# Window attention on one core: channel layout, GpSimd key sums, seeded PSUM banks

## Chip, cores and metric

The kernel runs on one core of one Trainium2 chip. The metric is device time in microseconds, from the launch to the end, median of three runs. PE is TensorE, DVE VectorE, ACT ScalarE, POOL GpSimd, SP the engine that issues most DMAs; all data is float32.

## What is computed

The input `x` has 4 images of 128 channels and 32x32 pixels. It is group-normalised (32 groups of 4 channels), goes through an attention over windows of 2x2 positions (8 heads of 16 features) on the image and on its 2x2 average pool, and is added to the result. The `reshape` reads the channel-first array as if it were channel-last, so a window's tokens come from several channels.

```python
def window_attn(x, Wqkv, bqkv, scale, ws=WS, nh=NH):
    B, H, W, C = x.shape
    hg, wg = (H // ws, W // ws)
    hd = C // nh
    xw = x.reshape(B, hg, ws, wg, ws, C).transpose(0, 1, 3, 2, 4, 5)
    qkv = (xw @ Wqkv + bqkv).reshape(B, hg * wg, ws * ws, 3, nh, hd)
    q, k, v = jnp.transpose(qkv, (3, 0, 1, 4, 2, 5))
    attn = jax.nn.softmax(jnp.einsum('bgnqd,bgnkd->bgnqk', q, k) * scale, axis=-1)
    o = jnp.einsum('bgnqk,bgnkd->bgnqd', attn, v)
...
g = window_attn(xr, Wqkv, bqkv, scale) @ Wproj + bproj
l = xr.reshape(B, C, H, W)
l = l.reshape(B, C, H // 2, 2, W // 2, 2).mean(axis=(3, 5))
l = l.reshape(B, h, w, C)
l = window_attn(l, Wqkv, bqkv, scale)
...
l = jax.image.resize(lx + ly, (B, C, H, W), method='bilinear')
l = l.reshape(B, H, W, C)
return (g + l).transpose(0, 3, 1, 2)
...
x = x + _L0_conv_ref(_gn(x), L0_conv_Wqkv, L0_conv_bqkv, L0_conv_Wproj, L0_conv_bproj)
```

`lx` and `ly` are averages of the low result with its neighbour row and neighbour column.

## The kernel before

The work is cut into ten tiles of 128 windows (`TILES`): two halves of each image, and two low tiles, `(None, 0)` and `(None, 1)`, each with the pooled maps of two images. A tile has 512 tokens: 4 token places of 128 windows. Token 0 is taken from the other three before the key and value products (softmax does not notice a shift common to all keys), so that only 3 keys need work; key 0's score is zero and its value is added whole.

Each engine runs a list written out by hand (`ORDER`), strictly in its order, with semaphore waits between engines. The steps, by name and line:

- Two row loads per image (`xr`, L285 to L290 and L419 to L422), and a second load of x by channels (`xc`, L295) for the addition at the end. SP issues most, ACT some.
- `bn`, `mean`, `dev`, `var`, `gvar`, `std`, `off`: statistics of each image's two row sets, group means by a small matmul, and the inverse deviation on POOL (L350).
- `scale` (ACT, L431) and `norm` (POOL, L278; DVE for image 0) make the normalised tokens `xn`, less token 0. `pool` (POOL, L373, L379) and `low` (ACT, L441) make the pooled ones.
- `xt` and `lt` (PE, L644, L656) turn a tile so that features lie on the partitions; `xto` and `lto` copy it out of PSUM.
- `Q`, `K`, `V` (PE, L681, L672, L691): products with the weights. `Qo` copies the queries out with their bias.
- `M` (DVE, L542): 4 queries times 3 keys for every window, 1536 elements for each partition. `S` (PE, L713) sums them over the heads for a batch of two tiles. `X` (DVE, L550, L555) takes the maximum off, `E` (ACT) is the exponential, `D` (DVE, L562 to L573) sums the denominators, inverts, multiplies and turns the weights in blocks.
- `P` (DVE, L590): weights times values, again 1536 elements.
- `v0` (PE, L739) turns key 0's value into a PSUM bank for each of the 4 queries, and `O` (PE, L755) adds the 12 products of 4 queries and 3 keys, each turned by a transposing matmul. `Oo` (ACT, L477) copies the sum out.
- `low` (PE, L771) is the resize matrix times the low result, 5 matmuls for half an image; `out` (PE, L778) adds the projection; `res` (ACT or DVE) adds the bias and, on DVE, x; `add` (POOL, L410) adds x where ACT did it. SP stores each image, the last one in two parts.

In the trace an fp32 matmul has two records, a transpose one.

## Time and profile before

| | us |
|---|---|
| median of 3 runs | 93.77 |
| lowest, highest | 93.16, 94.08 |
| span of the profiled execution | 92.3 |
| PE busy | 79.7 |
| DVE busy | 61.6 |
| ACT busy | 36.6 |
| POOL busy | 26.9 |

The span goes from the first to the last instruction on the core; the run's time includes what lies around it. The profiled execution's own total is not printed, so its span is set beside the median: 1.5 us lie between them. The busy shares are means over the whole span; the views that follow split them by stage. Line numbers are those of the kernel before.

### The profile page before, as it was taken

To read this page: it belongs to the slowest core of one execution; us is meant where nothing else is said; L and a number is where in the kernel's file an instruction comes from. 1 tells how busy PE (TensorE), PEld (TensorE's weight loads), DVE (VectorE), ACT (ScalarE), POOL (GpSimd) and SP (SyncE) were. 2 spreads that over 40 slices of the span, in tenths; PEclk is the share of its full clock that TensorE was granted. 3 is DMA by queue.
4 is the path that set the end of the run, shared out by engine and by line. 5 is a ranking of instruction groups with operands and counts; after the bars stand their busy time and mean duration, and the time that the engine had idled before them with its cause. 6 is when DMAs were issued, how large, how long until landed. Compare 5 with 4: busy or idle time off the path is not lost.

```text
span 92.3 us, 1700 instructions
## 1 busy us (share of the span) xinstructions
PE 79.7 (86%) x620; PEld 62.0 (67%) x620; DVE 61.6 (67%) x101; ACT 36.6 (40%) x80; POOL 26.9 (29%) x50
## 2 busy tenths in 40 slices
PE   1936057999999999999999999999999999999900
PEld 1925053878574577876677968797799897797500
DVE  0072499597685999999999918999779465003240
ACT  0050005577849997734564331331533150222000
POOL 6845595267364444000000000320060005060000
PEclk9999999999999999999999999999999999999999
DMA  0999999920000000000000000000005000005056
GB/s 6 248 254 251 228 322 404 415 87 0 7 0 0 0 4 0 11 0 0 0 0 0 7 0 0 0 0 0 7 0 227 0 0 4 7 0 227 0 227 227
DMA packets 3464, 7.32 MB, mean 79 GB/s; under 512 B 896, under 2 KB 1152, under 8 KB 3456
## 3 DMA queue, kind: packets, MB, share of 16 engines
q1 hardware_dynamic: 2592, 5.84, 18.4%
q10 hardware_dynamic: 864, 1.38, 6.3%
q8 instruction: 5, 0.08, 0.3%
q14 instruction: 3, 0.02, 0.1%
HBM read 5.11 MB, written 2.10 MB: 78 GB/s over the span
## 4 chain that ended last, share of the span: by engine, by line
PE 74%; DMA 9%; ACT 3%; POOL 3%; DVE 2%; issue 2%; ACTq 2%; DVEq 1%
PE ot_ps L755 14%; PE q_ps L681 9%; PE v_ps L691 9%; DMA xr<-in_x 9%; PE k_ps L672 6%; PE job_ps L771 6%; PE s_ps L713 6%; PE ot_ps L739 5%; PE job_ps L778 5%; PE job_ps L644 4%; PE k_ps L771 2%; ACT xn L431 2%; PE job_ps L656 2%; PE k_ps L778 2%; ACT xt L447 1%
## 5 line engine op out<-in xcount | busy, mean ns | idle before, releaser
L542 DVE TENSOR_TENSOR qk<-q_sb,k_ps 128x1536 f32<-128x1536 f32 x10 | 17.3, 1737 | 2.7 <-ACT q_sb L460 2.7
L410 POOL TENSOR_TENSOR out_sb<-out_sb,xc 128x512 f32<-128x512 f32 x4 | 6.0, 1512 | 40.9 <-ACT out_sb L482 40.9
L590 DVE TENSOR_TENSOR pv<-prob_w,v_ps 128x1536 f32<-128x1536 f32 x9 | 15.7, 1739 | 0.7 <-PE ot_ps L755 0.7
L755 PEld LDWEIGHTS ot_ps<-ident,pv 128*128 128x128 f32 x120 | 13.7, 141 | 3.3 <-issue 3.0
L755 PE MATMUL ot_ps<-ident,pv 128*128 128x128 f32 x120 | 14.9, 273 | 0.0
L477 ACT ACTIVATE ot<-ot_ps,bias_qkv 128x512 f32<-128x512 f32 x10 | 6.9, 687 | 12.8 <-PE ot_ps L755 12.8
L497 DVE BATCH_NORM_STATS2 bn<-xr 128x6 f32<-128x512 f32 x8 | 5.5, 682 | 6.6 <-DMA xr<-in_x 6.6
L681 PE MATMUL q_ps<-xt,w_sb 128*128 128x512 f32 x16 | 9.3, 665 | 0.5 <-ACT xt L447 0.5
L691 PEld LDWEIGHTS v_ps<-w_sb,xt 128*128 128x128 f32 x64 | 7.9, 192 | 1.0 <-issue 1.0
L691 PE MATMUL v_ps<-w_sb,xt 128*128 128x128 f32 x64 | 8.5, 275 | 0.0
L278 POOL TENSOR_TENSOR xn<-xn 128x384 f32<-128x384 f32 x6 | 6.0, 1000 | 8.0 <-ACT xn L431 8.0
L713 PE MATMUL s_ps<-qk,head_sum 128*32 128x192 f32 x160 | 7.5, 329 | 0.0
L431 ACT ACTIVATE xn<-xr,offset,rstd 128x256 f32<-128x256 f32 x12 | 6.6, 598 | 1.2 <-POOL offset L357 1.2
L672 PE MATMUL k_ps<-xt,w_sb 128*128 128x384 f32 x16 | 7.0, 517 | 0.0
L771 PEld LDWEIGHTS job_ps<-ot,resize_sb 128*128 128x128 f32 x50 | 6.1, 192 | 0.8 <-issue 0.8
L771 PE MATMUL job_ps<-ot,resize_sb 128*128 128x128 f32 x50 | 6.5, 277 | 0.0
L713 PEld LDWEIGHTS s_ps<-qk,head_sum 128*32 128x32 f32 x160 | 4.7, 110 | 2.6 <-issue 1.6
L739 PE MATMUL ot_ps<-ident,v_sb 128*128 128x128 f32 x40 | 6.1, 274 | 0.0
L599 DVE SCALAR_TENSOR_TENSOR out_sb<-k_ps,bias_p,xc 128x256 f32<-128x256 f32 x4 | 1.8, 480 | 6.4 <-PE k_ps L778 6.3
L644 PEld LDWEIGHTS job_ps<-ident,xn 128*128 128x128 f32 x28 | 3.6, 152 | 3.5 <-issue 1.5
L783 PE MATMUL q_ps<-ident 128*128 128x128 f32 x16 | 4.1, 440 | 1.9 <-POOL ident L317 1.9
L739 PEld LDWEIGHTS ot_ps<-ident,v_sb 128*128 128x128 f32 x40 | 4.7, 141 | 1.4 <-issue 1.4
(81 smaller groups left out, 120.3 us busy)
## 6 DMA issues: line engine op xcount, KB each, us to landing
xc<-in_x SPq DMA_DIRECT2D x4, 512.0 KB, 11.1
out<-out_sb SPq DMA_DIRECT2D x3, 512.0 KB, 2.6
xr<-in_x ACTq DMA_DIRECT2D x5, 256.0 KB, 8.0
xr<-in_x SPq DMA_DIRECT2D x3, 256.0 KB, 7.2
resize_sb<-in_resize SPq DMA_DIRECT2D x1, 640.0 KB, 9.1
out<-out_sb SPq DMA_DIRECT2D x2, 256.0 KB, 2.4
w_sb<-in_L_conv_Wqkv SPq DMA_DIRECT2D x1, 192.0 KB, 4.7
wp_sb<-in_L_conv_Wproj ACTq DMA_DIRECT2D x1, 64.0 KB, 8.9
```

The lines of the kernel that those rows point to most:

```text
L431: ins = nc.scalar.activation(xn[:, b, k, 2 * r:2 * r + 2, :].rearrange("p s f -> p (s f)"), xr[:, b, r, k * 256:(k + 1) * 256], ACT.Identi ...
L477: nc.scalar.activation(ot[:, n, :], ot_ps[:, :], ACT.Identity, bias=bias_qkv[:, 2:3]).then_inc(ot_out, 1)
L542: nc.vector.tensor_tensor(qk[:, m % 2, :, :, n % 2, :], q, k, ALU.mult).then_inc(qk_done, 1)
L590: nc.vector.tensor_tensor(to, p, v, ALU.mult).then_inc(pv_done, 1)
L644: ins = nc.tensor.transpose(bank(job)[:, j * P:(j + 1) * P], xn[:, b, k, j, :], ident[:, :])
L672: nc.tensor.matmul(k_ps[n % 2][:, 0:KEYS * NW], w_sb[:, C:2 * C], tokens(n)[:, NW:], start=True, stop=True).then_inc(k_made, 1)
L681: nc.tensor.matmul(q_ps[:, :], w_sb[:, 0:C], tokens(n), start=True, stop=True).then_inc(q_made, 1)
L691: ins = nc.tensor.matmul(v_ps[n % 2][:, j * C:(j + 1) * C], tokens(n)[:, j * NW:(j + 1) * NW], w_sb[:, 2 * C:], start=True, stop=True, ski ...
L713: ins = nc.tensor.matmul(s_ps[rows, 64:256], head_sum[:, q, :], qk[:, m % 2, q, :, :, rows], start=(q == 0), stop=(q == WIN - 1), skip_gro ...
L739: nc.tensor.matmul(view[:, q // 2, q % 2], v0_sb[:, n % V0BUF, :], eye, is_transpose=True, start=(q == 0), stop=False, skip_group_check=True)
L755: ins = nc.tensor.matmul(view[:, q // 2, q % 2], pv[:, n % 2, q, k, :], eye, is_transpose=True, start=(sums == KEYS and q == 0), stop=last ...
L771: nc.tensor.matmul(view[:, column // 4, column % 2], resize_sb[:, i, :], low_ot, start=(i == used[0]), stop=True, skip_group_check=True)
```

## The change

x is loaded once, by channels, one DMA for each image, all on SP's queue, and the normalised x stays in that layout. Statistics are per channel, then per group of 4 channels. The turned tiles get the token order on PE (`T`), token 0 is subtracted after the turn (`df`, on POOL for tiles 4 to 9, on DVE for tiles 0 to 3), and every tile has buffers of its own for tokens and queries. The order of tiles differs. Names of steps after: `st`/`ps`/`pw`/`of` statistics, `nm` normalise, `pn` pooled maps, `xe` copy of turned tokens, `oo`/`om` copies of turned sums, `L` resize, `W` projection, `R` result. `sum_keys` (`H`, POOL) adds the second and third key's products to the first; for the two low tiles a third addition brings key 0's value. `O` then turns 4 sums in place of 12 products; tile 9 has no `H` and turns 12. For the low tiles `Om` turns the middle of the sums again, and `L` needs 4 matmuls. Key 0's value goes into the output bank by an ACT copy (`sd`, two instructions) and x with the projection's bias by another (`sx`), ahead of the matmuls that accumulate there. At the start three 512-column matmuls (`mark_banks`) mark those banks as written. `D` of batches 0 to 3 is split: `Ds` (POOL) two additions, `Dr` (DVE) reciprocal, `D` (POOL) product, `U` (DVE) turn; batch 4's stays on DVE, with two additions in place of the reduction. PSUM is dealt out by two tables, `A_BANK` and `B_BANK`.

```diff
-TILES = [(0, 0), (0, 1), (1, 0), (None, 0), (1, 1), (2, 0), (None, 1), (2, 1), (3, 0), (3, 1)]
+TILES = [(0, 0), (None, 0), (0, 1), (1, 0), (1, 1), (None, 1), (2, 0), (2, 1), (3, 0), (3, 1)]
...
+A_BANK = {
+    ("st", 0): 1, ("st", 1): 0, ("st", 2): 2, ("st", 3): 2, ("T", 0): 0, ("Q", 0): 3, ("K", 0): 0, ("T", 1): 1,
+    ("Q", 1): 3, ("K", 1): 2, ("V", 0): 2, ("V", 1): 3, ("O", 1): 1, ("Om", 1): 0, ("T", 2): 1, ("Q", 2): 1,
+    ("K", 2): 2, ("T", 3): 3, ("Q", 3): 3, ("K", 3): 0, ("V", 2): 2, ("V", 3): 0, ("T", 4): 1, ("Q", 4): 3,
+    ("K", 4): 1, ("T", 5): 1, ("Q", 5): 0, ("K", 5): 0, ("V", 4): 2, ("V", 5): 1, ("O", 5): 1, ("Om", 5): 2,
+    ("T", 6): 2, ("Q", 6): 1, ("K", 6): 0, ("T", 7): 1, ("Q", 7): 3, ("K", 7): 0, ("V", 6): 2, ("V", 7): 0,
+    ("T", 8): 3, ("Q", 8): 1, ("K", 8): 0, ("T", 9): 3, ("Q", 9): 2, ("K", 9): 3, ("V", 8): 1, ("V", 9): 3,
+}
+B_BANK = {
+    ("sd", 0): 1, ("sd", 2): 1, ("sd", 3): 1, ("sd", 4): 2, ("sd", 6): 0, ("sd", 7): 2, ("sd", 8): 2, ("sd", 9): 0,
+    ("sx", 0, 0): 2, ("sx", 0, 1): 0, ("sx", 1, 0): 0, ("sx", 1, 1): 1, ("sx", 2, 0): 1, ("sx", 2, 1): 2,
+    ("sx", 3, 0): 0, ("sx", 3, 1): 1,
+}
+PV = [2, 1, 3, 0, 0, 2, 3, 1, 3, 0]
+PV_BUFS = 1 + max(PV)
+ORDER = {
+    "PE": [
+        ("st", 0), ("st", 1), ("st", 3), ("T", 3), ("T", 2), ("T", 0), ("Q", 3), ("st", 2), ("T", 1), ("K", 3),
+        ("Q", 0), ("Q", 2), ("K", 2), ("zero",), ("K", 0), ("T", 4), ("Q", 1), ("S", 1), ("K", 1), ("T", 7), ("V", 3),
+        ("T", 9), ("T", 5), ("T", 6), ("T", 8), ("S", 0), ("V", 2), ("Q", 4), ("K", 4), ("Q", 5), ("Q", 7), ("Q", 9),
+        ("K", 5), ("V", 1), ("Q", 8), ("V", 0), ("S", 2), ("O", 2), ("K", 8), ("K", 9), ("Q", 6), ("V", 4), ("Om", 1),
+        ("O", 1), ("O", 3), ("K", 7), ("V", 5), ("S", 4), ("O", 0), ("V", 9), ("K", 6), ("L", 0, 1), ("L", 0, 0),
+        ("W", 0, 1), ("W", 0, 0), ("S", 3), ("V", 8), ("Om", 5), ("L", 1, 1), ("L", 1, 0), ("O", 4), ("W", 1, 0),
+        ("V", 7), ("W", 1, 1), ("O", 5), ("O", 9), ("O", 8), ("L", 3, 1), ("V", 6), ("W", 3, 1), ("L", 3, 0),
+        ("O", 7), ("W", 3, 0), ("L", 2, 0), ("L", 2, 1), ("O", 6), ("W", 2, 1), ("W", 2, 0),
+    ],
+    "DVE": [
+        ("bn", 0), ("bn", 1), ("ag", 0), ("ag", 1), ("ps", 0), ("ps", 1), ("bn", 3), ("of", 1), ("ag", 3), ("of", 0),
+        ("nm", 0, 0), ("bn", 2), ("df", 3), ("ag", 2), ("ps", 3), ("df", 2), ("df", 0), ("of", 3), ("ps", 2),
+        ("df", 1), ("of", 2), ("M", 3), ("M", 2), ("M", 0), ("X", 1), ("M", 1), ("Dr", 1), ("U", 1), ("P", 3),
+        ("X", 0), ("P", 2), ("Dr", 0), ("M", 4), ("U", 0), ("M", 5), ("P", 1), ("P", 0), ("M", 8), ("X", 2), ("M", 9),
+        ("M", 7), ("Dr", 2), ("X", 4), ("U", 2), ("P", 5), ("M", 6), ("P", 4), ("D", 4), ("U", 4), ("X", 3), ("P", 8),
+        ("Dr", 3), ("P", 9), ("U", 3), ("P", 7), ("P", 6), ("R", 3, 0),
+    ],
+    "ACT": [
+        ("sx", 0, 1), ("nm", 1), ("nm", 0, 1), ("xe", 3), ("pn", 1), ("xe", 2), ("pn", 0), ("xe", 0), ("Qo", 3),
+        ("xe", 1), ("pn", 3), ("pn", 2), ("Qo", 0), ("Qo", 2), ("nm", 3), ("xe", 4), ("nm", 2), ("Qo", 1), ("E", 1),
+        ("xe", 7), ("xe", 9), ("xe", 5), ("ve", 3), ("xe", 8), ("xe", 6), ("ve", 2), ("E", 0), ("Qo", 4), ("sd", 2),
+        ("Qo", 5), ("Qo", 7), ("Qo", 9), ("ve", 1), ("ve", 0), ("Qo", 8), ("sx", 0, 0), ("oo", 2), ("sd", 3),
+        ("Qo", 6), ("om", 1), ("oo", 1), ("oo", 3), ("E", 2), ("ve", 5), ("ve", 4), ("sd", 0), ("oo", 0),
+        ("sx", 1, 1), ("ve", 9), ("E", 4), ("R", 0, 0), ("sd", 4), ("R", 0, 1), ("sx", 1, 0), ("ve", 8), ("E", 3),
+        ("oo", 4), ("om", 5), ("R", 1, 0), ("sd", 8), ("ve", 7), ("sd", 9), ("R", 1, 1), ("oo", 5), ("sx", 3, 1),
+        ("oo", 8), ("oo", 9), ("sx", 3, 0), ("ve", 6), ("sd", 7), ("R", 3, 1), ("sx", 2, 0), ("oo", 7), ("sx", 2, 1),
+        ("sd", 6), ("oo", 6), ("R", 2, 1), ("R", 2, 0),
+    ],
+    "POOL": [
+        ("p1", 0), ("p2", 0), ("p1", 1), ("p2", 1), ("pw", 0), ("pw", 1), ("p1", 3), ("p2", 3), ("p1", 2), ("p2", 2),
+        ("keyb",), ("pw", 3), ("pw", 2), ("df", 4), ("Ds", 1), ("df", 7), ("D", 1), ("df", 5), ("df", 9), ("df", 8),
+        ("Ds", 0), ("df", 6), ("D", 0), ("H", 2, 0), ("H", 2, 1), ("H", 3, 0), ("H", 3, 1), ("H", 1, 0), ("H", 1, 1),
+        ("H", 1, 2), ("H", 0, 0), ("H", 0, 1), ("Ds", 2), ("D", 2), ("H", 5, 0), ("H", 5, 1), ("H", 5, 2),
+        ("H", 4, 0), ("H", 4, 1), ("Ds", 3), ("H", 8, 0), ("D", 3), ("H", 8, 1), ("H", 7, 0), ("H", 7, 1),
+        ("H", 6, 0), ("H", 6, 1),
+    ],
+}
+STORES = [0, 1, 3, 2]
+WARM = {("st", 0): 4, ("T", 0): 6}
...
         def _(sp):
-            sp.dma_start(xr[:, 0, 0, :], x_rows[0, 0]).then_inc(x0_first, 16)
+            sp.dma_start(xc[:, 0, :], x_chan[0]).then_inc(x_loaded[0], 16)
             sp.dma_start(w_sb[:, :], w_qkv).then_inc(w_loaded, 16)
-            for r in range(2):
-                sp.dma_start(xr[:, 2, r, :], x_rows[2, r]).then_inc(x_loaded[2], 16)
+            for b in range(1, B):
+                sp.dma_start(xc[:, b, :], x_chan[b]).then_inc(x_loaded[b], 16)
             for a in range(3):
                 sp.dma_start(bias_qkv[:, a:a + 1],
                              b_qkv[a * C:(a + 1) * C].rearrange("(p a) -> p a", a=1)).then_inc(bias_loaded, 16)
             sp.dma_start(bias_p[:, :], b_proj.rearrange("(p a) -> p a", a=1)).then_inc(bp_loaded, 16)
+            for h in range(2):
+                at = 2 * C + (1 - h) * 64
+                sp.dma_start(bias_mid[h * 64:(h + 1) * 64, :],
+                             b_qkv[at:at + 64].rearrange("(p a) -> p a", a=1)).then_inc(mid_loaded, 16)
+            sp.dma_start(wp_sb[:, :], w_proj).then_inc(wp_loaded, 16)
...
                 for k in range(2):
-                    result_written(sp, b, k)
+                    result_read(sp, b, k)
...
+            def less_token_0(n):
+                pool.wait_ge(token_0_out, nth("ACT", ("xe", n)))
+                rest = xt[:, n, NW:].rearrange("f (j w) -> f j w", j=KEYS)
+                nc.gpsimd.tensor_tensor(rest, rest, xt[:, n, 0:NW].unsqueeze(1).broadcast_to([P, KEYS, NW]),
+                                        ALU.subtract).then_inc(inputs_made[n], 1)
+            def denominators(m):
+                pool.wait_ge(exp_done, nth("ACT", ("E", m)))
+                done = nth("POOL", ("Ds", m))
+                e = expd[:, m % 2, :]
+                nc.gpsimd.tensor_tensor(pair_sum[:, m % 2, :], e[:, 0:128], e[:, 128:256], ALU.add).then_inc(pair_pool, 1)
+                pool.wait_ge(pair_pool, done)
+                nc.gpsimd.tensor_tensor(denom[:, m % 2, :], pair_sum[:, m % 2, 0:64], pair_sum[:, m % 2, 64:128],
+                                        ALU.add).then_inc(denom_pool, 1)
+            def divide(m):
+                pool.wait_ge(inv_pool, nth("DVE", ("Dr", m)))
+                if m >= 2:
+                    pool.wait_ge(turn_done, 2 * nth("DVE", ("U", m - 2)))
+                nc.gpsimd.tensor_tensor(prob[:, m % 2, :].rearrange("r (k w) -> r k w", k=KEYS),
+                                        expd[:, m % 2, 64:].rearrange("r (k w) -> r k w", k=KEYS),
+                                        inv[:, m % 2, :].unsqueeze(1).broadcast_to([P, KEYS, 64]),
+                                        ALU.mult).then_inc(prob_made[m], 1)
+            def sum_keys(n, i):
+                if i == 0:
+                    pool.wait_ge(pv_done, nth("DVE", ("P", n)))
                 else:
...
+            def scale_image(b, k=None):
+                act.wait_ge(offset_done, nth("DVE", ("of", b)))
+                at = (lambda t: t[:, b, :]) if k is None else (lambda t: halves(t, b, k))
+                nc.scalar.activation(at(xn), at(xc), ACT.Identity, bias=offset[:, b:b + 1],
+                                     scale=rstd[:, b:b + 1]).then_inc(normed_act, 1)
...
+            def value_0_out(n):
+                act.wait_ge(v_made, nth("PE", ("V", n)))
+                bank = a_bank(("V", n))
+                if is_low(n):
+                    nc.scalar.copy(v0[:, n, :], bank[:, KEYS * C:]).then_inc(v0_out, 1)
+                else:
+                    act.wait_ge(bias_loaded, 48)
+                    nc.scalar.activation(v0[:, n, :], bank[:, KEYS * C:], ACT.Identity,
+                                         bias=bias_qkv[:, 2:3]).then_inc(v0_out, 1)
+            def value_0_seed(n):
+                act.wait_ge(v0_out, nth("ACT", ("ve", n)))
+                b_free(act, ("sd", n))
+                to = b_bank(("sd", n))[:, :].rearrange("f (s m r c) -> f s m r c", s=2, r=2, c=GROUP)
+                at = v0[:, n, :].rearrange("f (m c) -> f m c", c=GROUP)
+                for s in range(2):
+                    ins = nc.scalar.copy(to[:, s], at.unsqueeze(2).broadcast_to([P, 32, 2, GROUP]))
+                ins.then_inc(seeded, 1)
...
+            def input_seed(b, k):
+                act.wait_ge(x_loaded[b], 16)
+                act.wait_ge(bp_loaded, 16)
+                b_free(act, ("sx", b, k))
+                nc.scalar.activation(b_bank(("sx", b, k))[:, :].rearrange("f (s h c) -> f s h c", s=2, h=2),
+                                     result_part(xc, b, k), ACT.Identity, bias=bias_p[:, 0:1]).then_inc(x_seeded, 1)
...
+            def less_token_0(n):
+                dve.wait_ge(token_0_out, nth("ACT", ("xe", n)))
+                nc.vector.tensor_tensor(xt[:, n, NW:].rearrange("f (j w) -> f j w", j=KEYS),
+                                        a_bank(("T", n))[:, NW:].rearrange("f (j w) -> f j w", j=KEYS),
+                                        xt[:, n, 0:NW].unsqueeze(1).broadcast_to([P, KEYS, NW]),
+                                        ALU.subtract).then_inc(inputs_made[n], 1)
...
             def divide(m):
+                dve.wait_ge(exp_done, nth("ACT", ("E", m)))
+                done = nth("DVE", ("D", m))
+                e = expd[:, m % 2, :]
+                nc.vector.tensor_tensor(pair_sum[:, m % 2, :], e[:, 0:128], e[:, 128:256], ALU.add).then_inc(pair_done, 1)
+                dve.wait_ge(pair_done, done)
+                nc.vector.tensor_tensor(denom[:, m % 2, :], pair_sum[:, m % 2, 0:64], pair_sum[:, m % 2, 64:128],
                                         ALU.add).then_inc(denom_done, 1)
+                dve.wait_ge(denom_done, done)
                 nc.vector.reciprocal(inv[:, m % 2, :], denom[:, m % 2, :]).then_inc(inv_done, 1)
+                dve.wait_ge(inv_done, done)
                 nc.vector.tensor_tensor(prob[:, m % 2, :].rearrange("r (k w) -> r k w", k=KEYS),
+                                        e[:, 64:].rearrange("r (k w) -> r k w", k=KEYS),
                                         inv[:, m % 2, :].unsqueeze(1).broadcast_to([P, KEYS, 64]),
+                                        ALU.mult).then_inc(prob_made[m], 1)
+            def invert(m):
+                dve.wait_ge(denom_pool, nth("POOL", ("Ds", m)))
+                if m >= 2:
+                    dve.wait_ge(prob_made[m - 2], 1)
+                nc.vector.reciprocal(inv[:, m % 2, :], denom[:, m % 2, :]).then_inc(inv_pool, 1)
+            def turn_weights(m):
+                dve.wait_ge(prob_made[m], 1)
                 for half in range(2):
                     nc.vector.transpose(
                         prob_w[:, m % 2, half, :].rearrange("w (q k h) -> w k q h", q=WIN, k=KEYS),
                         prob[:, m % 2, :].rearrange("r (k t w) -> r t k w", k=KEYS, t=2)[:, half]).then_inc(turn_done, 1)
...
+            def mark_banks():
+                for bank in b_ps:
+                    ins = nc.tensor.matmul(bank[:, :], ident[:, :], ident[:, :].unsqueeze(1).broadcast_to([P, 4, P]),
+                                           start=True, stop=True, skip_group_check=True)
+                ins.then_inc(banks_marked, 1)
+            def keep_warm(n):
+                for _ in range(n):
+                    nc.tensor.matmul(s_ps[:, 64:64 + P], ident[:, :], ident[:, :], start=True, stop=True,
+                                     skip_group_check=True)
...
+            def sum_values(n):
+                sums = [j for j in among("POOL", "H") if j[1] == n]
+                if sums:
+                    pe.wait_ge(keys_summed, nth("POOL", sums[-1]))
+                else:
+                    pe.wait_ge(pv_done, nth("DVE", ("P", n)))
+                left = [0] + list(range(1 + min(len(sums), 2), KEYS))
+                if is_low(n):
+                    a_free(pe, ("O", n))
+                    view = a_bank(("O", n))[:, :].rearrange("f (i l a r c) -> f r l i a c", i=2, l=KL, a=8, r=2)
                     eye = ident[:, :].rearrange("p (i a c) -> p i a c", i=2, a=8)
                 else:
+                    pe.wait_ge(seeded, nth("ACT", ("sd", n)))
+                    view = b_bank(("sd", n))[:, :].rearrange("f (s m r c) -> f r s m c", s=2, m=32, r=2)
+                    eye = ident[:, :].rearrange("p (m c) -> p m c", c=GROUP)
                 for q in range(WIN):
+                    for k in left:
+                        part = low_sum[:, TILES[n][1], q * C:(q + 1) * C] if is_low(n) else pv[:, PV[n], q, k, :]
+                        ins = nc.tensor.matmul(view[:, q // 2, q % 2], part, eye, is_transpose=True,
+                                               start=(is_low(n) and q == 0), stop=(k == left[-1]), skip_group_check=True)
+                ins.then_inc(ot_made, 1)
...
+                pe.wait_ge(x_seeded, nth("ACT", ("sx", b, k)))
+                pe.wait_ge(ot_out, nth("ACT", ("oo", low)))
+                pe.wait_ge(mid_out, nth("ACT", ("om", low)))
+                for h in range(2):
+                    for s in range(2):
+                        j = 4 * h + 2 * k + s
+                        if FIRST[j] == 64:
+                            values_at = mid[:, b // 2, b % 2 * P:(b % 2 + 1) * P]
+                        else:
+                            at = b % 2 * 256 + FIRST[j]
+                            values_at = ot[:, low, at:at + P]
+                        at = s * 256 + h * P
+                        nc.tensor.matmul(b_bank(("sx", b, k))[:, at:at + P], resize_sb[:, j, :], values_at, start=False,
+                                         stop=True, skip_group_check=True)
```

## Rows read from the trace of the kernel before

**Rows 1.** Busy us (count) of PE, PEld, DVE, ACT, POOL, then clock; 18 to 88.

```profile
span 92.3 us, 1700 instructions
18.00:88.00 70.00, 69.80 (x578) 54.08 (x578) 51.98 (x74) 32.68 (x73) 16.07 (x18) 1.00 0.06 22
```

**Rows 2.** Chain of work that ended last, PE's pieces: start us, us, records.

```profile
38.40 0.44 PE ot_ps L739 x4
38.83 0.86 PE q_ps L681 x2
39.70 0.65 PE k_ps L672 x2
40.34 1.31 PE ot_ps L755 x12
41.65 0.89 PE v_ps L691 x8
...
43.84 1.44 PE s_ps L713 x32
...
69.95 1.12 PE job_ps L771 x10
```

**Rows 3.** Timeline, DVE within 39 to 47 us: start us, us, instruction.

```profile
39.27 0.55 DVE L565 RECIPROCAL inv<-denom 128x64 f32<-128x64 f32 x1
...
40.25 0.44 DVE L573 STREAM_TRANSPOSE prob_w<-prob 128x96 f32<-128x96 f32 x2
...
40.62 3.38 DVE L542 TENSOR_TENSOR qk<-q_sb,k_ps 128x1536 f32<-128x1536 f32 x2
...
45.58 0.41 DVE L550 TENSOR_REDUCE row_max<-s_ps 128x64 f32<-128x256 f32 x1
```

**Rows 4.** POOL's two-input operations: busy and mean ns, or by line (min/median/max).

```profile
L278 POOL TENSOR_TENSOR xn<-xn 128x384 f32<-128x384 f32 x6 | 6.0, 1000 | 8.0 <-ACT xn L431 8.0
L373 POOL TENSOR_TENSOR rows<-xr x4: 1038/1039/1434, 5.8 to 19.0; 128x512 f32<-128x512 f32 x4
L410 POOL TENSOR_TENSOR out_sb<-out_sb,xc x4: 1507/1512/1519, 59.1 to 81.5; 128x512 f32<-128x512 f32 x4
```

**Rows 5.** DVE's products by line (min/median/max ns), and DVE beside POOL in time.

```profile
L542 DVE TENSOR_TENSOR qk<-q_sb,k_ps x10: 1714/1741/1755, 20.1 to 61.8; 128x1536 f32<-128x1536 f32 x10
L590 DVE TENSOR_TENSOR pv<-prob_w,v_ps x9: 1715/1742/1755, 32.9 to 70.9; 128x1536 f32<-128x1536 f32 x9
11.95 0.56 DVE L278 TENSOR_TENSOR xn<-xn 128x384 f32<-128x384 f32 x1
...
14.37 0.73 POOL L379 TENSOR_TENSOR pooled<-rows 128x256 f32<-128x256 f32 x1
...
14.40 1.12 DVE L278 TENSOR_TENSOR xn<-xn 128x384 f32<-128x384 f32 x1
```

**Rows 6.** ACT's copies and activations, groups by form.

```profile
L477 ACT ACTIVATE ot<-ot_ps,bias_qkv 128x512 f32<-128x512 f32 x10 | 6.9, 687 | 12.8 <-PE ot_ps L755 12.8
L447 ACT COPY xt<-job_ps 128x512 f32<-128x512 f32 x7 | 4.1, 580 | 3.1 <-PE job_ps L644 2.9
L466 ACT COPY v_sb<-v_ps 128x128 f32<-128x128 f32 x10 | 2.6, 261 | 6.0 <-PE v_ps L691 6.0
```

**Rows 7.** The start: bytes moved in 40 slices; first statistics, Q and M by time.

```profile
GB/s 6 248 254 251 228 322 404 415 87 0 7 0 0 0 4 0 11 0 0 0 0 0 7 0 0 0 0 0 7 0 227 0 0 4 7 0 227 0 227 227
...
5.66 0.69 DVE L497 BATCH_NORM_STATS2 bn<-xr 128x6 f32<-128x512 f32 x1 [0.23 <-DMA xr<-in_x]
...
8.60 0.73 POOL L350 TENSOR_TENSOR rstd<-gvar,half_pow 128x2 f32<-128x2 f32 x1 [0.97 <-DVE gvar L516]
...
14.44 2.05 PE L681 MATMUL q_ps<-xt,w_sb 128*128 128x512 f32 x2 [0.47 <-ACT xt L447]
...
20.08 1.74 DVE L542 TENSOR_TENSOR qk<-q_sb,k_ps 128x1536 f32<-128x1536 f32 x1
```

**Rows 8.** Timeline, the last DMA issues after DVE's last result.

```profile
88.93 0.83 SPq L306 DMA_DIRECT2D out<-out_sb  x2
```

748 lines of the change are left out of this document (302 added, 446 removed), and 18 rows, old and new, of the table ORDER.

## The prediction

> **What bounds the kernel now.** First the busy times by stretch. From 18 to 88 us PE is busy 69.80 of 70.00 us, DVE 51.98, ACT 32.68, POOL 16.07 [rows 1]: look for the engine with no idle time. Then the chain that ended last, which in this stretch is PE's pieces one behind another; it gives PE's price for each step [rows 2]: turning key 0's value (v0) 0.44, Q 0.86, K 0.65, turning the products (O) 1.31, V 0.89, S 1.44, resize 1.12. So in the middle only PE counts, and every microsecond taken from it is gained until the next engine is full. That is DVE, with 52 us in the same stretch; the middle can therefore not give back all that PE loses. Last, the start (first M at 20.08 [rows 7]) and the end (last store issued at 88.93, 3.4 us before the end of the span [rows 8]) are latency and have to be costed apart.
>
> **PE's work.** Before, by [rows 2]: Q 10 x 0.86 = 8.6, K 6.5, V 8.9, S 5 x 1.44 = 7.2, O 13.1, v0 4.4, resize 8 x 1.12 = 9.0, projection 8 x 0.86 = 6.9, turning tokens 8 x 0.44 and 2 x 0.89 = 5.3: 69.9, which is what the stretch shows. After: Q, K, V, S and projection as before (38.1). O turns 4 sums for 9 tiles at v0's price for four (4.0) and 12 products for tile 9 (1.3); Om 2 x 0.22 = 0.4; v0 goes; resize 4 matmuls in place of 5, 8 x 0.90 = 7.2; turns 10 x 0.44 = 4.4. Sum 55.4, 14.5 less. The new turns write runs of 4 elements; O already does so, with 1.31 for twelve, no dearer for each than v0's four.
>
> **DVE's work from its first M.** Two M in a row take 3.38, so 1.69 each [rows 3]; M and P are 20 of these, 33.6. X is two operations of 0.41 and its like, 0.8, five times: 4.0. A reciprocal 0.59 with its hand-off, four in `Dr`: 2.4. Two turns 0.37 (40.25 to 40.62 [rows 3]), five times: 1.9. D of batch 4 stays whole: its two additions replace a reduction at about its price, 1.5 in all. Sum 43.4.
>
> **POOL's new work.** No row shows a 512-element addition in this form. Pro rata from 384 elements in 1000 ns it is 1.33; the 512-element one with scattered output takes 1.51, the one that reads x in pairs 1.04 [rows 4]. I take 1.30, with 0.08 to the next one that waits for it: 1.38 each, bounds 1.04 and 1.51. Twenty are 27.6. `Ds` is 0.8 (192 elements in two parts), `D` 0.6, by the same proportion and a small fixed part; four batches 5.6. Six `df` 1.0 each. Some 39 us from about 26 on: it fits beside DVE, if it isn't late.
>
> **Does POOL hold DVE up?** DVE's 384-element subtraction with two operands in SBUF took 0.56 at 11.95, but 1.12 at 14.40, while POOL worked from 14.37 to 15.10. M and P, whose second operand is in PSUM, stayed within 1714 to 1755 over the whole run, and POOL's addition at 1507 to 1519 beside them [rows 4, 5]. So M, P and X run beside `H` unharmed; `D` of batch 4, with three DVE operations on two SBUF operands, falls in the middle of POOL's `H` for tiles 5 and 4. Each waits for the rest of one, half of 1.3 on average, which is 2.0; I take 1.5, bounds 0 and 3.9. The Trainium skill (SBUF — State Buffer, "SBUF: two separate sides") says that the pair of ports VectorE and GpSimd share is an exclusive lock for a whole instruction, wanted by VectorE operations with two SBUF inputs or in a two-port mode. By that page D pays up to three full waits, 80.5 becoming about 83; the trace agrees for the one pair of operations that overlapped there.
>
> **The walk.** In-order queues make the sum a walk; I took each wait from the lists.
> - Start. Transfers of 2 KB rows ran at about 250 GB/s, the later ones of 4 KB rows at 404 to 415 [rows 7]. x0's second half came at 5.66, after 0.23 of waiting; alone on the engines and in 4 KB rows the whole of it (512 KB) is due about a microsecond earlier, 4.5; x1 then at 6.2, the last image near 9. Two statistics of 0.69 each for x1 end at 7.6. From the end of the last statistics of image 0 to its inverse deviation took 3.0 before (5.66 + 0.69 to 8.60 + 0.73 [rows 7]), so 10.7 with both images; offset, after image 3's statistics on DVE, 11.7; ACT scales image 1 in 1.24 (0.85 for 1024 elements, the rest fixed) to 12.9. Then turn, copy, subtraction, six warming matmuls, Q, turn, K, about 7.3 with cold PE (Q took 2.05 at 14.44 against 0.86 later [rows 2, 7]): first M 20.2. One load fewer gains nothing here; before, DVE itself was the late one.
> - M, M, M, X, M to 28.0, with 0.3 lost waiting for queries. `Dr` to 28.6, POOL's `D` to 29.4, `U` to 29.85: DVE idles 0.8.
> - P, X, P, Dr, M, U, M, P, P, M, X, M, M: 9 x 1.69 + 1.6 + 0.6 + 0.4, to 47.6. POOL ends `D` of batch 0 at 35.3, nine `H` at 47.7, `Ds` of batch 2 at 48.5: DVE waits 0.9, `Dr` 49.1.
> - X, U, P, M, P to 55.4; D 1.5 and 1.5 of waits, 58.4; U, X, P 61.2; Dr, P, U, P 65.6, with POOL's `D` in time between two `H`.
> - Last tile. `V` of tile 6 stands in PE's queue behind `O` of tiles 9 and 8 and a resize part. P of tile 9 ends at 63.5, its twelve turns at 64.8, then 0.44, 0.9, 0.89: 67.1; ACT's copy 67.5. DVE idles 1.9; the last P ends at 69.2.
> - Tail. Two `H` 2.8, O 0.44, ACT's copy 0.58, projection 0.86, ACT's result 0.6, hand-offs: 74.8. Store and end as before, 3.4: span 78.2.
>
> To the median I add the 1.5 between it and the profiled span: 79.7. The walk leaves out small hand-offs, some twelve of 0.06 on the path: 80.5.
>
> ACT gets 8 seeds of two copies, 256 elements each, 0.37 (0.83 ns for an element and 0.155 fixed, from 580 and 261 ns [rows 6]): 6; 8 of x at 0.69: 5.5; 4 more results: 2.4. With what remains it has some 34 us in the 54 from first M to end. It costs nothing while the bank it seeds is free early; without cover each seed is 0.7 on the path.
>
> **Rivals.** *POOL sets the pace.* With `H` at 1.51 the ninth ends 1.9 later, DVE waits for `Ds` 2.8, the last two add 0.4, and D's three waits grow by 2: 84 to 85. For it: the one 512-element row with two whole operands. Against: the 384-element row, contiguous like `H`. *PE goes cold.* With 14.5 us of work gone PE idles about 15% of the middle. In the stretch where it never idled the granted clock was 1.00 [rows 1], and Q took 0.86; the first Q, after a start with idle time, took 2.05 [rows 2, 7], a ratio of 2.4 and so no faster than the lower of the levels 2.4 and 1.2 GHz would have it. Ten microseconds of PE work at half speed, half of it on the path, cost 5, with all on it 10: 85 to 90. Against: waits are mostly under 1 us. *PE's queue eats the gain.* Each step waits in a fixed list for DVE, POOL and ACT in turn; if the waits sum to the 14.5 us, 93 to 94 (most of that chance is within 1%). Against: two such waits alone show in the walk, 0.9 and 1.9. *The two engines take turns.* If each POOL operation shut DVE out whatever its operands, 33 us of `H`, `Ds` and `D` would go in series with DVE's 43.4: 20.2 + 76.6, tail and ends 11.2, 108: slower. It decides from 14 us of the 33 on. Against: M's and P's even times.
>
> **Chances.** The walk as it is (77.5 to 83) 0.66; POOL sets the pace 0.17; PE cold 0.10; PE's queue eats it 0.03; taking turns 0.04. Low end: no waits in D (1.5) and `H` at 1.04, which takes DVE's wait and 0.5 of the tail away (1.5): 77.5. High end 86, with POOL's pace and a part of the cold PE. Within 1% is what a measurement here can't tell from no change: 0.02. Faster by more 0.94, slower by more 0.04.
>
> **What the profile would show.** PE busy near 60 in the span with gaps; 52 turning matmuls for O; M and P still 1.74; `H` at 1.3; first M at 20; DVE waiting at `Dr` of batch 2 and before tile 6's P; D's three operations each longer than alone; last P at 69. I am wrong if `H` is over 1.5 or delays M and P, if Q passes 0.9 mid-run, or if the first M comes after 22.

## The result, and the profile after

The changed kernel takes 86.56 us (median of 4 runs, 85.92 to 86.70) where the kernel before, run beside it, takes 93.70 (93.16 to 94.08): a ratio of 0.9225, 95% interval 0.9179 to 0.9270. It is faster, by 7.1 us where 13.2 were forecast; the time lies 0.56 above the upper end of the range. The profiled execution took 85.92, with a span of 84.1, so 1.8 lie outside the span. Here and below, medians are over all executions of a kernel, while ratios and intervals leave out those that came out over 1.5% above its fastest.

The page of the changed kernel, its busy times and five of the lines in 40 slices (of 2.1 us each; PEclk is the granted clock in tenths):

```profile
span 84.1 us, 1464 instructions
PE 69.6 (83%) x494; PEld 49.2 (59%) x494; DVE 59.7 (71%) x94; ACT 51.2 (61%) x97; POOL 48.9 (58%) x69
PE   0996304999999999999999999999879779976900
DVE  0066899934989887999998989999999960850000
ACT  0000099703898567586195675907949999996750
PEclk9999995557999999999999999999999999999999
GB/s 29 344 295 370 286 49 0 0 0 0 0 0 8 0 0 4 0 0 0 12 0 0 0 0 0 8 0 4 0 249 0 0 185 64 0 0 249 8 23 226
```

Two things stand out against [rows 1]. PE has idle time in slices 4 to 7 of the start, and from slice 7 on its granted clock is at half for three slices. And ACT, 36.6 us busy before, is busy for 51.2, with hardly a gap in slices 31 to 36; the forecast summed its work but did not expect it to be full there.

Stretches of the changed kernel (start:end, length, busy of PE, PEld, DVE, ACT, POOL with counts, granted clock, DMA share, GB/s):

```profile
10.00:15.00 5.00, 1.33 (x6) 1.22 (x6) 4.90 (x16) 4.34 (x4) 4.60 (x6) 0.79 0.17 57
15.00:20.00 5.00, 5.00 (x23) 4.75 (x22) 2.54 (x11) 1.79 (x5) 0.75 (x3) 0.52 0.00 0
20.00:65.00 45.00, 44.09 (x373) 30.82 (x372) 41.95 (x54) 30.76 (x66) 29.47 (x33) 1.00 0.04 13
65.00:70.00 5.00, 3.85 (x29) 3.09 (x28) 3.54 (x4) 5.00 (x11) 3.80 (x4) 1.00 0.26 105
70.00:75.00 5.00, 4.56 (x30) 3.28 (x29) 2.48 (x2) 4.77 (x8) 2.55 (x2) 1.00 0.00 0
```

Groups of instructions of the changed kernel (busy us, mean ns of one | idle before them and its releaser), which answer to [rows 4, 5, 6]:

```profile
L403 POOL TENSOR_TENSOR pv<-pv 128x512 f32<-128x512 f32 x18 | 23.0, 1282 | 7.1 <-DVE pv L613 6.4
L613 DVE TENSOR_TENSOR pv<-prob_w,a_ps 128x1536 f32<-128x1536 f32 x10 | 17.4, 1745 | 3.5 <-ACT v L454 3.3
L553 DVE TENSOR_TENSOR qk<-q_sb,a_ps 128x1536 f32<-128x1536 f32 x10 | 17.4, 1745 | 1.1 <-ACT q_sb L439 0.4
L487 ACT ACTIVATE b_ps<-xc,bias_p 128x512 f32<-128x512 f32 x8 | 9.6, 1206 | 0.6
L492 ACT COPY out_sb<-b_ps 128x512 f32<-128x512 f32 x7 | 7.6, 1103 | 2.8 <-PE b_ps L780 2.8
```

`H` (L403) takes 1.28 and the products 1745 ns, as before with POOL beside them. The seeds of x (L487, `sx`) take 1.21 and the results (L492, `R`) 1.10, where the forecast had 0.69 and 0.6.

DVE's timeline of the changed kernel (start us, us, instruction, [idle before <- releaser]): x1's statistics, the first M, the four operations of `D` of batch 4, and the last two P.

```profile
7.10 1.29 DVE L505 BATCH_NORM_STATS2 bn<-xc 128x6 f32<-128x512 f32 x2 [1.63 <-DMA xc<-in_x]
...
22.24 1.75 DVE L553 TENSOR_TENSOR qk<-q_sb,a_ps 128x1536 f32<-128x1536 f32 x1
...
57.80 0.98 DVE L574 TENSOR_TENSOR pair_sum<-expd 128x128 f32<-128x128 f32 x1
58.81 1.19 DVE L576 TENSOR_TENSOR denom<-pair_sum 128x64 f32<-128x64 f32 x1
60.03 0.55 DVE L579 RECIPROCAL inv<-denom 128x64 f32<-128x64 f32 x1
60.62 0.85 DVE L581 TENSOR_TENSOR prob<-expd,inv 128x192 f32<-128x192 f32 x1
...
66.82 1.75 DVE L613 TENSOR_TENSOR pv<-prob_w,a_ps 128x1536 f32<-128x1536 f32 x1
71.87 1.75 DVE L613 TENSOR_TENSOR pv<-prob_w,a_ps 128x1536 f32<-128x1536 f32 x1 [3.29 <-ACT v L454]
```

ACT's timeline of the changed kernel ahead of that last P:

```profile
66.38 1.14 ACT L492 COPY out_sb<-b_ps 128x512 f32<-128x512 f32 x1
67.27 0.71 ACT L471 ACTIVATE ot<-a_ps,bias_qkv 128x512 f32<-128x512 f32 x1
67.83 1.24 ACT L487 ACTIVATE b_ps<-xc,bias_p 128x512 f32<-128x512 f32 x1
68.94 1.12 ACT L474 COPY ot<-b_ps 128x512 f32<-128x512 f32 x2
70.18 1.20 ACT L487 ACTIVATE b_ps<-xc,bias_p 128x512 f32<-128x512 f32 x1
71.31 0.35 ACT L454 ACTIVATE v<-a_ps,bias_qkv 128x128 f32<-128x128 f32 x1
71.56 0.68 ACT L464 COPY b_ps<-v 128x256 f32<-128x256 f32 x2
```

DVE waits 3.29 us for the 0.35 us copy of tile 6's values at 71.31. ACT has no gap ahead of it: the copy stands behind two seeds and a result of 1.1 to 1.2 each. It could not have come sooner on PE's side either. PE's rows, a resize part and the end of `V` of tile 6:

```profile
69.17 0.46 PE L773 MATMUL b_ps<-ot,resize_sb 128*128 128x128 f32 x2 [0.61 <-issue]
...
70.80 0.39 PE L697 MATMUL a_ps<-xt,w_sb 128*128 128x128 f32 x2
```

The resize part starts 0.10 behind the end of the seed of 67.83 (at 69.07), which it needs, and `V`, next in PE's list, ends at 71.19. So ACT's length reaches DVE in two ways, through its own list and through PE's wait for a seed.

**Where the walk and the trace part.** The forecast's walk beside the trace, by DVE's marks:

| mark | walk | trace | behind | of it new |
|---|---|---|---|---|
| first M starts | 20.2 | 22.24 | 2.0 | 2.0 |
| P of tile 4 ends | 55.4 | 57.88 | 2.5 | 0.4 |
| P of tile 8 ends | 61.2 | 64.37 | 3.2 | 0.7 |
| P of tile 7 ends | 65.6 | 68.57 | 3.0 | -0.2 |
| last P starts | 67.5 | 71.87 | 4.4 | 1.4 |
| last result ends | 74.8 | 81.05 | 6.2 | 1.9 |

So a third of the loss lies ahead of the first M, 0.7 in `D` of batch 4, and over half after P of tile 7, where ACT is full. For the experiments I therefore read two lengths from each profile: the start of the first M, and from it to the end of ACT's last result, here called the body. Here they are 22.24 and 58.8 (81.05 less 22.24); the walk had 20.2 and 54.6.

### The profile page after: what moved, and what is told of

It reads as the page before. It is cut to its first block, busy times and chain, and to the rows that moved or that the text cites. A ratio compares the mean times of both kernels' runs of the same rounds, so it can differ in the third digit from the quotient of the medians.

```text
span 84.1 us, 1464 instructions
## 1 busy us (share of the span) xinstructions
PE 69.6 (83%) x494; PEld 49.2 (59%) x494; DVE 59.7 (71%) x94; ACT 51.2 (61%) x97; POOL 48.9 (58%) x69
## 4 chain that ended last, share of the span: by engine, by line
PE 34%; POOL 16%; DVE 15%; ACT 10%; issue 9%; DMA 6%; SPq 5%; DVEq 0%; ACTq 0%; POOLq 0%
POOL pv L403 9%; DMA bias_p<-in_L_conv_bproj 6%; PE b_ps L773 5%; PE a_ps L678 4%; PE a_ps L668 4%; PE b_ps L742 4%; PE s_ps L720 4%; PE a_ps L683 3%; DVE pv L613 3%; PE b_ps L780 3%; PE s_ps L638 3%; ACT out_sb L492 2%; SPq L307 2%; POOL xt L370 2%; DVE qk L553 2%
## 5 line engine op out<-in xcount | busy, mean ns | idle before, releaser
L403 POOL TENSOR_TENSOR pv<-pv 128x512 f32<-128x512 f32 x18 | 23.0, 1282 | 7.1 <-DVE pv L613 6.4
L613 DVE TENSOR_TENSOR pv<-prob_w,a_ps 128x1536 f32<-128x1536 f32 x10 | 17.4, 1745 | 3.5 <-ACT v L454 3.3
L553 DVE TENSOR_TENSOR qk<-q_sb,a_ps 128x1536 f32<-128x1536 f32 x10 | 17.4, 1745 | 1.1 <-ACT q_sb L439 0.4
L773 PE MATMUL b_ps<-ot,resize_sb 128*128 128x128 f32 x48 | 8.1, 281 | 2.5 <-issue 2.5
L487 ACT ACTIVATE b_ps<-xc,bias_p 128x512 f32<-128x512 f32 x8 | 9.6, 1206 | 0.6
L678 PE MATMUL a_ps<-xt,w_sb 128*128 128x512 f32 x20 | 9.9, 601 | 0.0
L492 ACT COPY out_sb<-b_ps 128x512 f32<-128x512 f32 x7 | 7.6, 1103 | 2.8 <-PE b_ps L780 2.8
L691 PEld LDWEIGHTS a_ps<-w_sb,xt 128*128 128x128 f32 x60 | 7.8, 191 | 2.7 <-issue 2.4
L691 PE MATMUL a_ps<-w_sb,xt 128*128 128x128 f32 x60 | 8.5, 278 | 0.0
L683 PE MATMUL a_ps<-xt,w_sb 128*128 128x384 f32 x20 | 8.2, 498 | 0.0
L780 PE MATMUL b_ps<-ot,wp_sb 128*128 128x512 f32 x16 | 8.0, 598 | 0.0
```

The source lines that it names most:

```text
L403: nc.gpsimd.tensor_tensor(to, first, other, ALU.add).then_inc(keys_summed, 1)
L487: nc.scalar.activation(b_bank(("sx", b, k))[:, :].rearrange("f (s h c) -> f s h c", s=2, h=2), result_part(xc, b, k), ACT.Identity, bias=b ...
L492: nc.scalar.copy(result_part(out_sb, b, k), b_bank(("sx", b, k))[:, :].rearrange("f (s h c) -> f s h c", s=2, h=2)).then_inc(res_act, 1)
L553: nc.vector.tensor_tensor(scores_slot(m)[:, :, :, n % 2, :], q, k.unsqueeze(1).broadcast_to(shape), ALU.mult).then_inc(qk_done, 1)
L613: nc.vector.tensor_tensor(pv[:, PV[n], :, :, :].rearrange("w q k (h d) -> w q (k h) d", d=HD), p, v, ALU.mult).then_inc(pv_done, 1)
L678: nc.tensor.matmul(a_bank(("Q", n))[:, :], w_sb[:, 0:C], xt[:, n, :], start=True, stop=True).then_inc(q_made, 1)
```

## The experiments

The theories. A: `sx` and `R` walk xc and out_sb (in SBUF) one element (4 bytes) in every eight and so cost ACT 1.1 to 1.2 each, and ACT sets the pace of the end. B: the place of `V` of tile 6 in PE's queue does. C: PE at the low clock delays the first M. D: batch 4's `D` on DVE, which waits for POOL. E: the key sums on POOL are a gain, as the forecast said. Every time below is the median, with the ratio to the kernel before, run beside it, and its interval; "body" and "first M" are from the profile.

### The order of ScalarE's walks (A)

```diff
+def result_pairs(t, b, k): return t[:, b, :].rearrange("f (c h k s) -> f k c h s", h=2, k=2, s=2)[:, k]
+def bank_pairs(bank): return bank[:, :].rearrange("f (s h c) -> f c h s", s=2, h=2)
-  activation(bank.rearrange("f (s h c) -> f s h c", s=2, h=2), result_part(xc, b, k), ...)
+  activation(bank_pairs(bank), result_pairs(xc, b, k), ...)      # the same for R on ACT and on DVE
```

> Same work as the changed kernel; only the order in which ACT's eight input seeds and seven results (and DVE's one) walk over the half image differs: pairs of neighbouring pixels instead of steps of eight. Theory A (the end of the changed kernel runs at ACT's pace, because these copies take 1.2 and 1.1 us in place of the 0.69 and 0.6 I had put down): each falls to 0.7 to 0.75, ACT's busy time falls from 51 to about 44, the last P starts 1 to 2 us earlier, and the time falls by 3 to 4, to 82.5 to 83.5. Theory B (the end is held by PE's list: the values of tile 6 stand behind the turned sums of tiles 9 and 8): the copies may get faster but the last P still starts near 70 to 71 and the time falls by less than 1.5.

82.94 (0.882, 0.877 to 0.888), 3.6 less. By line (min/median/max ns):

```profile
L494 ACT ACTIVATE b_ps<-xc,bias_p x8: 720/740/778, 12.7 to 72.7; 128x512 f32<-128x512 f32 x8
L498 ACT COPY out_sb<-b_ps x7: 607/625/663, 56.6 to 77.4; 128x512 f32<-128x512 f32 x7
```

and DVE's last P in its timeline:

```profile
70.33 1.75 DVE L618 TENSOR_TENSOR pv<-prob_w,a_ps 128x1536 f32<-128x1536 f32 x1 [2.34 <-ACT v L461]
```

The same elements move, now in an order that takes two neighbours of xc together (and jumps between the halves of the bank for it), and a seed costs 740 ns in place of 1200, a result 625 in place of 1102. ACT's busy time falls from 51.2 to 44.6. The body falls by 2.5 to 56.3; the first M comes 0.56 earlier (one seed, `sx` 0, 1, stands ahead of the scaling of image 1 on ACT; but the start moves by as much from one execution to another). A holds, as the largest cause.

The order in pairs is the one that the kernel before has. Its results on ACT, not among [rows 6], have a row of their own:

```profile
L482 ACT ACTIVATE out_sb<-job_ps,bias_p 128x512 f32<-128x512 f32 x4 | 2.9, 734 | 3.0 <-PE job_ps L778 3.0
```

It walks out_sb as "f (m k s) -> f k m s", two neighbours together, in 734 ns. The change rewrote this order for its new layout of the bank, and the diff shows it.

### A warm TensorE at the start (C)

```diff
-WARM = {("st", 0): 4, ("T", 0): 6}
+WARM = {("st", 0): 7, ("st", 3): 14, ("T", 3): 3, ("T", 0): 6}
```

> 17 more filler matmuls on PE between the first statistics and the first turned tile, so that PE does not idle from 7.7 to 14.3 us. Theory C (the late first M, 22.2 in place of 20.2, comes from PE's clock, granted 0.52 of full from 15 to 20 us after that idle time): the clock stays at 1.00 in every stretch, the first Q pair takes 0.86, the first M comes at 20.0 to 20.5 and the time falls by 1.5 to 2, to about 84.8. Rival (the start is held by the chain of statistics, not by PE's pace): first M stays within 0.7 of 22.2 and the time within 1.

84.39 (0.898, 0.893 to 0.903), 2.2 less. Seventeen more matmuls on the identity fill PE's idle time between 7.7 and 14.3, and three more stand behind the first turned tile. The stretch:

```profile
15.00:20.00 5.00, 4.86 (x34) 3.92 (x34) 4.37 (x19) 3.35 (x10) 1.50 (x4) 1.00 0.01 3
```

and the first M in DVE's timeline:

```profile
20.53 1.75 DVE L553 TENSOR_TENSOR qk<-q_sb,a_ps 128x1536 f32<-128x1536 f32 x1
```

The granted clock is 1.00 where it was 0.52 (the 2.4 GHz level in place of 1.2), and twelve equal small matmuls there take 1.50 us where they took 2.77. The first M starts 1.7 earlier; the body, 58.8, has not moved. C holds. The fillers are no guarantee, though: of the seven profiles of kernels with this list of fillers, three (e6, e13, e14) have a granted clock of 0.67 to 0.71 in 10 to 15 us all the same, and a first M at 21.4 to 21.9.

### V of tile 6 earlier (B), and batch 4's denominators (D)

```diff
 PE:  ("V", 7), ("W", 1, 1), +("V", 6),  ("O", 5), ("O", 9), ("O", 8), ("L", 3, 1), -("V", 6)
 ACT: ("ve", 7), ("sd", 9), +("ve", 6), ("R", 1, 1), ... ("sx", 3, 0), -("ve", 6)
```

> The values of tile 6 are computed on PE ahead of the turned sums of tiles 5, 9 and 8, and their copy stands further up in ACT's list; the products of tile 6 go to another of the four product buffers. Theory B: the last P follows the one before it at 68.5 in place of 71.9, POOL's last two additions follow it, and the time falls by 2.4 or more, to about 84. Theory A: the last P comes 3 us earlier, but the seeds and results on ACT still stand one behind another, and the time falls by less than 1.

86.20 (0.918, 0.912 to 0.924), body 58.9. The last P now follows the one before at once (66.96 for both), 3.2 earlier than in the changed kernel, and the end doesn't move: the wait of 3.29 in front of it was where ACT's lateness showed, not its cause. B falls as the cause of the changed kernel's end.

```diff
-  tensor_tensor(pair_sum, e[:, 0:128], e[:, 128:256], ALU.add); tensor_tensor(denom, pair_sum[:, 0:64], ...)
+  tensor_reduce(denom, e.rearrange("r (k w) -> r w k", k=WIN), AX.X, ALU.add)      # D of batch 4, on DVE
```

> The softmax of the last batch on DVE sums its denominators by one reduction (one operand, as in the kernel before) in place of two additions with two operands in SBUF. Theory D (each two-operand addition waits for POOL's addition that runs beside it): the part that took 0.98 + 1.19 falls to 0.60, the product with the inverses keeps its wait (0.85 or up to 1.6), so the stage on DVE gets 1 to 1.6 us shorter. The time falls by 0.5 to 1.5 if DVE's chain counts there, by nothing if the end is set by ACT. Rival (these operations are slow in themselves): the reduction takes no less than 2 us.

86.02 (0.913, 0.906 to 0.920), body 58.75. `D` and its turn take 2.7 instead of 4.1 (reduction 0.64, product 1.00), and the last P waits 3.98 in place of 3.29. What DVE gained there, it lost again waiting for the values that ACT copies out. D as a cost of the changed kernel falls.

### Both mends together, and the end once more

> Both edits at once: pair order in the seeds and results, and filler matmuls in the start. If theories A and C name separate costs, their gains add: 86.56 less 3.6 (86.56 to 82.94) less 2.2 (86.56 to 84.39) is 80.8, which is also what the prediction had (80.5). If the gain of the one was the same waiting as the gain of the other, 82 or more.

The edits of A and C together: 81.53 (0.866, 0.860 to 0.870), 5.0 less than the changed kernel, with first M at 20.01 and a body of 56.3. The single gains were 3.6 and 2.2, together 5.8; the median lies between the 80.8 of separate costs and the 82 of one and the same. In the profile they are separate: the first M is e2's (20.53) or better, the body is e1's (56.3). With B's edit on top:

> As before this, and the values of tile 6 ahead of the turned sums of tiles 5, 9 and 8, with another product buffer. Alone that edit gave 0.4 or nothing, though the last P started 3 us earlier: ACT's list took it up. Theory A+B: with ACT's copies at 0.7 the list no longer takes it up, DVE doesn't wait before the last P (2.3 in the run with pair order), and the time falls by another 1 to 2, to about 79.3. Rival: PE's own list of resize parts and projections is full from 65 us to the end, and the gain is under 0.7.

80.85 (0.859, 0.853 to 0.864), 0.7 less by the median, with intervals that overlap, and a body of 55.7, 0.6 less. Now that ACT is relieved, the earlier `V` is worth something, but not the 1 to 2 expected; the rival named under 0.7, for a PE list that is full to the end. With the reduction, no `H` for tile 6, and `R` of the last image's first half on DVE on top:

```diff
 DVE:  ("P", 6), ("R", 3, 0), +("R", 2, 0)         ACT: ("R", 2, 1), -("R", 2, 0)
 POOL: ("H", 7, 1), -("H", 6, 0), -("H", 6, 1)
```

> All at once: pair order, filler matmuls, tile 6's values early, one reduction in the last batch's softmax, the last tile without key sums (12 turned products, 0.87 us more on PE, for two additions of POOL, 2.6 us, less on the path), and the last result copied by DVE beside ACT's. Expected below the run without the last three edits by 1.5 to 3, about 77. If PE's list is what holds the end, below 1.

81.14 (0.862, 0.858 to 0.867), where 1.5 to 3 less were expected: nothing gained. The body as measured, to the end of ACT's last result, falls to 54.8, but that is the measure: the last result is now DVE's.

```profile
75.65 0.69 DVE L620 COPY out_sb<-b_ps 128x512 f32<-128x512 f32 x1 [4.48 <-PE b_ps L780]
```

It ends at 76.34, 55.9 behind the first M (20.42), where e6 had its last result 55.7 behind. Bodies from here on compare with one another (they all lack these 1.1 us), not with the ones above or with the walk's 54.6.

### Without the key sums (E)

```diff
 POOL: -("H", 2..3, 0..1), -("H", 0, 0..1), -("H", 4, 0..1), -("H", 8, 0..1), -("H", 7, 0..1), -("H", 6, 0..1)
```

> The changed kernel with POOL's key sums of the seven image tiles taken out (14 of its 20 additions; those of the two low tiles stay): PE turns 12 products in place of 4 sums, 0.87 us more for each of seven tiles, 6.1 in all. Theory E (PE is without slack from 20 to 60 us, and POOL's additions are hidden there): four tiles' 3.5 us are paid in full, three tiles' 2.6 in the end are set off by POOL's two additions in a row (2.6 us) that no longer stand before the last turn: 88 to 90. Rival (the additions' latency costs as much as they save): 85 to 87.

90.41 (0.960, 0.952 to 0.968), 3.9 more than the changed kernel (88 to 90 were expected), PE busy 76.1 and a body of 63.2. The sums are worth their place on POOL. The run also gives `D` of batch 4 with POOL idle from 60.96 on. In the changed kernel POOL's rows beside `D` are:

```profile
57.34 1.29 POOL L403 TENSOR_TENSOR low_sum<-pv,v 128x512 f32<-128x512 f32 x1
58.58 2.68 POOL L403 TENSOR_TENSOR pv<-pv 128x512 f32<-128x512 f32 x2
```

Here POOL's last operation ahead of it, and DVE's timeline:

```profile
59.68 1.28 POOL L402 TENSOR_TENSOR low_sum<-pv,v 128x512 f32<-128x512 f32 x1
```

```profile
60.15 0.96 DVE L573 TENSOR_TENSOR pair_sum<-expd 128x128 f32<-128x128 f32 x1
61.15 0.23 DVE L575 TENSOR_TENSOR denom<-pair_sum 128x64 f32<-128x64 f32 x1
61.41 0.55 DVE L578 RECIPROCAL inv<-denom 128x64 f32<-128x64 f32 x1
61.99 0.36 DVE L580 TENSOR_TENSOR prob<-expd,inv 128x192 f32<-128x192 f32 x1
```

The first addition ends at 61.11, 0.15 behind the end of POOL's at 60.96; the other two take 0.23 and 0.36, and in the changed kernel, with `H` beside them, 1.19 and 0.85. The reciprocal, with one operand, is 0.55 in both.

### The loads

```diff
 # changed kernel (e10), and e8 with the warming ("Q", 3): 2 in place of ("T", 0): 6 (e9)
+sp.dma_start(bias_p ...)   # moved from behind the images' loads to just behind w_sb, ahead of x1
```

> The run with all edits, and two more in the start: the projection's bias is loaded right behind the weights, so that ACT's first seed no longer waits for it until 10.5 to 11.4 us ahead of the first normalisation; and four of the six fillers ahead of the third turned tile go, the other two stand behind it. Theory F (from the first M to the end PE is the engine without slack once ACT's copies are short: 20.4 to 75.6 us with 55 us of work): what the start gains reaches the end one for one. First M at 19.0 to 19.6, time 79.7 to 80.3. Rival (some chain through DVE and POOL sets the end): the start gains, the end doesn't, 80.7 or more.

> The changed kernel, with one edit: the projection's bias is loaded right behind the weights. It tells how much of the late start is the seed that stands first in ACT's list and waits for this load. Theory: image 1's normalisation starts at about 12.4 in place of 13.04, the first M comes 0.6 earlier, and the time falls by 0.3 to 0.7. Rival (PE's low clock sets the first M whatever ACT does): nothing, within 0.3.

e9 81.51 (0.869, 0.860 to 0.877) and e10 86.43 (0.925, 0.919 to 0.931): nothing gained in either, where 79.7 to 80.3 and 0.3 to 0.7 less were expected. ACT's seed is done early now and the scaling of image 1 waits for its offset, since x1's statistics start later: at 8.51 and 8.75, where the twelve profiles with the old order of loads (e12 to e14 with them) have them between 7.1 and 8.3. That 0.5 KB ahead of x1 costs x1 about what the seed gains fits these two executions; it is not shown apart from the spread.

```diff
-x0, w_sb, x1, x2, x3
+x0, x1, w_sb, x3, x2        # e11, on e8 with the warming of e9; e15: and bias_p right behind x1
```

> The run with all edits and the shifted fillers, with the projection's bias where the changed kernel loads it, and the loads in the order x0, x1, weights, x3, x2: nothing stands between the first two images. In the runs so far image 1's statistics begin between 7.1 and 8.1 us, at 8.5 and 8.75 where the small load of the bias stood ahead of x1; the walk had 6.2. If the 192 KB of weights ahead of x1 hold it up, it comes 0.5 earlier, at about 7.2, the first M at 19.5 or less (20.4 in the run with all edits), and, by the theory that PE has no slack from there on, the time falls by 0.5 to 1, to about 80.3. Rival (what holds x1 is not the bytes ahead of it): statistics at 7.7 to 8.1 and no gain.

> The fastest so far (79.82: loads in the order x0, x1, weights, x3, x2), with the projection's bias loaded right behind x1. In that run ACT's first seed waited for the bias until 11.5, so that image 1's normalisation started at 13.45 though its offset was there at 11.9. Expected: normalisation at 12.1 to 12.5, first M 19.0 in place of 19.7, time 79.0 to 79.5. If the small load holds up what is behind it as it did ahead of x1 (0.7 us), image 3's statistics come later and the gain is nil.

e11 79.82 (0.850, 0.844 to 0.856) and e15 79.53 (0.848, 0.840 to 0.856). In e11 the statistics of both images run back to back, and the first M comes at 19.67; the bodies (54.7, 54.8) are those of e8. The two can't be told apart.

```profile
4.00 2.67 DVE L510 BATCH_NORM_STATS2 bn<-xc 128x6 f32<-128x512 f32 x4 [4.00 <-DMA xc<-in_x]
```

### What holds the end of the mended kernel

Five kernels each take away work and nothing else (e12 to e14 on e8, e16 and e18 on e15); what they leave out is missing in their output. The expectations call theories by letters again: F, PE alone sets the end; G, one other list alone does (DVE's in e13, ACT's in e16); H, I and J in the words given there. Theory H has nothing to do with the step `H`.

```diff
+  if h == 0:  matmul(bank, resize_sb[:, j, :], ...)              # e12: half of the resize matmuls
+  q = slice(0, 2 if n >= 4 else 4); tensor_tensor(pv[:, q], ...)  # e13: P of six tiles halved; e14: both
+  c = slice(0, 64 if b >= 2 else P)                               # e16: the seeds of images 2, 3 halved; e18: e16 and e12
```

> The run with all edits, but the resize takes two of its four matmuls for each half image: the lower or upper rows of the low result are left out, so the output isn't the reference's. PE has 8 x 0.45 = 3.6 us less work, 2.7 of it after 55 us. Theory F (PE sets the time from first M to the end once ACT's copies are short): the time falls by 2.5 to 3.6, to 77.5 to 78.6. Rival (the chain P, POOL, turn, projection sets the end): under 1.

> The run with all edits (81.14), but for tiles 4 to 9 DVE makes the products of weights and values for two of the four queries (the other two keep what an earlier tile left in the buffer, so the output isn't the reference's): six P of about 0.95 in place of 1.74, 4.8 us less on DVE, all of it after 50 us. Taking 3.6 us off PE had given 0.5. Theory G (DVE's list alone sets the end): the time falls by 3.5 or more, to 77.5. Theory H (PE and DVE are both full from 20 us on, and either holds the end when the other is relieved): the time falls by less than 1.5.

> The run with all edits, with both reliefs: half of the resize's matmuls (3.6 us less on PE) and half of six tiles' products (4.8 us less on DVE). Theory H: together they give clearly more than the sum of what each gives alone, 2.5 to 4 us, to 77 to 78.5. If a third thing (ACT's seeds, POOL's additions, the order of the lists) holds the end, no more than the sum of the two.

> The fastest version so far (pairs, warming, batch 4's denominators by a reduction, x in the new order, the small load behind x1) with ACT relieved at its end alone: the seeds of x for images 2 and 3 write half of their bank, so x is left out of half of those images' output, and what this computes isn't the reference's. Each of the four seeds costs ACT some 0.33 less (0.74 to about 0.41), 1.3 in all, all of it after 60 us. Theory G (in the mended kernel ACT's list of seeds and copies sets the end): the last seed of values ends up to 1.3 earlier and so does the span; the time is 78.3 to 79.0 against 79.5 to 79.8 of the same kernel beside it. Theory H (ACT is busy but not late: the last turn waits for TensorE's resize parts or VectorE's last product): time within 0.3 of the other.

> The fastest version again, unchanged, as the measure for the kernel with the half seeds, on the same chip: 79.5 to 79.8, ratio 0.848 to 0.851 to the kernel before.

> The kernel with half seeds (the fastest version, with the four seeds of x for images 2 and 3 writing half of their bank) with half of the resize matmuls left out too: both ScalarE and TensorE relieved; neither x nor the low resolution is whole in the output, so what this computes isn't the reference's. From the first M to the end of ScalarE's last result the fastest version took 54.73 to 54.76, ScalarE relieved 54.57 (0.2 less), and on its parent TensorE relieved 54.40 (0.4 less). Theory I (the two lists are equally long there and hand banks to each other, so one relieved alone runs into the other): more than the sum of the two, over 0.8, up to 1.3, so 53.4 to 53.9, and a time of 78.1 to 78.6. Theory J (neither holds the end; the last turn waits for something else, VectorE's copies or the banks): the sum or less, 54.1 to 54.6, a time of 78.8 to 79.3.

| kernel | relieved | median, ratio [95%] | first M | body |
|---|---|---|---|---|
| e8 | | 81.14, 0.862 [0.858, 0.867] | 20.42 | 54.84 |
| e12 | PE | 80.61, 0.859 [0.854, 0.864] | 20.19 | 54.40 |
| e13 | DVE | 81.28, 0.866 [0.858, 0.874] | 21.86 | 54.85 |
| e14 | PE and DVE | 79.81, 0.852 [0.846, 0.859] | 21.77 | 53.68 |
| e17 (e15 again) | | 79.47, 0.845 [0.840, 0.849] | 18.24 | 54.73 |
| e16 | ACT | 79.10, 0.841 [0.836, 0.845] | 19.11 | 54.57 |
| e18 | ACT and PE | 78.93, 0.837 [0.833, 0.841] | 18.61 | 53.99 |

(The late first M of e13 and e14 goes with the lower granted clock of 10 to 15 us named above; from 20 us on it is 1.00.) Relieving PE by 3.6 us of work gives 0.4, DVE nothing, ACT (four seeds, 0.74 to 0.50 each) 0.2, PE and DVE together 1.2, ACT and PE together 0.7. F as it was meant (a gain one for one) falls, and so does G, for DVE and for ACT.

The trace says more than the sums. In e8 PE is busy 51.57 of the 51.86 us from the first M to the last turn (72.28), and in e17 51.47 of 51.74: PE is the engine without slack there. In e12 it is busy 48.68 of 51.38, so that of 2.9 us of work less only 0.5 show, and 2.4 more are waits. The largest, 1.2, is for POOL:

```profile
59.19 0.66 PE L742 MATMUL b_ps<-ident,pv 128*128 128x128 f32 x4 [1.23 <-POOL pv L409]
```

POOL adds the keys of tiles 5 and 4 in five operations one behind another from 52.56 to 59.13, right behind P of tile 5, and PE's turn of tile 4 needs the last. It starts 39.0 us behind the first M, in e8 39.2. In e18 the same wait is 1.23 again, in e14, where P of tile 4 is halved too, 0.68, and the turn comes 38.3 behind the first M; that is most of what PE and DVE together gain. Of the chain that ended last POOL has 17% in e8, 25% in e12 and 27% in e18. So POOL's key sums are the first thing behind PE. No run relieves POOL alone or POOL and PE, and what that would give is open.

Behind that turn ACT is next. ACT's last steps in e12:

```profile
68.77 0.72 ACT L493 ACTIVATE b_ps<-xc,bias_p 128x512 f32<-128x512 f32 x1
69.43 0.57 ACT L480 COPY ot<-b_ps 128x512 f32<-128x512 f32 x1
70.12 0.72 ACT L493 ACTIVATE b_ps<-xc,bias_p 128x512 f32<-128x512 f32 x1
70.77 0.67 ACT L470 COPY b_ps<-v 128x256 f32<-128x256 f32 x2
```

ACT goes from copy to copy, PE has waited 0.52 and 0.66 for it, and the last turn on PE starts behind the seeds of values ending at 71.44. In e16, ACT relieved, the same seeds wait instead, for a result that DVE copies out of their bank. DVE's row, and ACT's:

```profile
69.06 0.69 DVE L623 COPY out_sb<-b_ps 128x512 f32<-128x512 f32 x1 [3.50 <-PE b_ps L783]
```

```profile
69.84 0.68 ACT L471 COPY b_ps<-v 128x256 f32<-128x256 f32 x2 [0.45 <-DVE out_sb L623]
```

In e16 PE's list has no gap from 65.7 to the last turn at 70.67. With both relieved (e18), gaps come up on PE, small ones, each for a hand-off; PE's timeline:

```profile
65.10 1.10 PE L784 MATMUL b_ps<-ot,wp_sb 128*128 128x512 f32 x2 [0.75 <-ACT ot L481]
...
68.69 0.46 PE L777 MATMUL b_ps<-ot,resize_sb 128*128 128x128 f32 x2 [0.31 <-issue]
...
69.58 1.50 PE L745 MATMUL b_ps<-ident,pv 128*128 128x128 f32 x12 [0.21 <-ACT b_ps L471]
```

0.74 in the body is more than 0.2 and 0.4 added, as theory I has it, but short of the 0.8 that it named, and the medians (78.93 and 79.47) don't settle it. What the rows show is that PE's list is full, and that a PE relieved by 2.9 us runs first into POOL's key sums and then into ACT's copies and seeds, with a chain of hand-offs (turn, ACT's copy, projection, result, seed of the bank, turn) hardly shorter behind them. How much each of these is worth is left open; relieved alone, none of PE, DVE and ACT is worth more than 0.45.

## Why the prediction was right in direction and short in size

**Right.** *PE's saving.* 14.5 were forecast. From its first turned tile on, without fillers and statistics, PE is busy 59.5 where the kernel before has 73.3: 13.8 less. (Both lie some 3.5 to 4 above the forecast's sums, 55.4 and 69.9, which left out the slow start; [rows 1]'s stretch, which the 69.9 was said to match, begins behind the first turns and the first Q.) The turns are the 52 forecast, 48 for `O` and 4 for `Om`. *`H`.* 1.30 was taken between 1.04 and 1.51 [rows 4]; it is 1.28, and POOL is not late: `Dr` of batch 2 ends at 51.44, with no wait for POOL, where the walk had one of 0.9. That rival's price of 1.51 came from a row with scattered output, which `H` has not. *Beside one another.* M and P stay at 1694 to 1755 with POOL busy, as [rows 5] said; the engines do not take turns. *Key sums pay:* e7. DVE's sum has a slip without weight: 20 products of 1.69 are 33.8, not 33.6. Of the signs of being wrong one came, the first M after 22.

**`D` of batch 4, a term sized short.** Forecast 1.5 of waits; measured, against e7's rows with POOL idle, 0.96 (1.19 less 0.23), 0.49 (0.85 less 0.36), and some 0.7 in the first, an estimate, since no row has it alone; its end follows the end of POOL's by 0.15. Together about 2.2. Three operations with two operands in SBUF, three waits for the rest of a POOL instruction. The Trainium skill (SBUF — State Buffer, "SBUF: two separate sides") describes an exclusive lock on the ports that the two engines share, held for the length of an instruction. By that rule the trace agrees in the mechanism, but none of the waits was a full 1.28, which had given 3.9. It cost less than it measured: two of the three taken away (e4), the time went into the wait ahead of the last P.

**ACT, the step that failed.** "It costs nothing while the bank it seeds is free early", and before it, "8 of x at 0.69", "4 more results: 2.4". The prices were of activations and copies that walk contiguous elements [rows 6], and even the kernel before's own results, in pairs, took 734; the change's own walk of xc and out_sb, f (c h k s) in the order s h c, steps from one element to another with gaps. That stands in the diff, and was not priced: 1.20 and 1.10, 15 of them, 7.6 us more than forecast. And it wasn't only busy time off the path: the forecast summed ACT over 54 us (34 of them busy) and never walked it. From 60 us on ACT's list is dense: results, seeds and turned products fall together there, and PE waits for seeds (0.54 and 0.61 at 66.62 and 69.17). The stretches show ACT (in 65 to 75) busy for 5.00 and 4.77 of 5 us where PE has 3.85 and 4.56. The tail has a term sized short too: two results stand one behind another there, where the walk had one of 0.6.

```profile
78.97 2.08 ACT L492 COPY out_sb<-b_ps 128x512 f32<-128x512 f32 x2 [0.28 <-PE b_ps L780]
```

Of the body's 4.2 us above the walk, the order of the walks gave back 2.5 (e1), and `V`'s place another 0.6 once ACT was relieved (e6). The remaining 1.1 no run gave back: the reduction and the shorter tail did not (e8). What they are is open.

**The start, 2.0 late.** Two parts. The first turn on PE starts at 14.26 in the trace, 1.4 behind the walk's 12.9. x1 was due at 6.2 and came at 7.1, though x0 came at 4.18, 0.3 early: the 704 KB of w_sb and x1 took 2.9 us where the walk had 1.7, at the 404 to 415 GB/s of [rows 7]; the page's slices of that time show 295 to 370. And the seed of x on ACT (ready to start at 10.56, when bias_p had landed, with 1.28 for its table and 1.19 for itself) held up the scaling of image 1 to 12.98, where its offset was there at 12.4. With x1 ahead of w_sb it is there by 5.6 (e11, e15), and the first M comes 0.75 earlier in e11 than in e8, which is within what the start moves by itself. The second part is PE: from first turn to first M the walk had 7.3, taken from the kernel before with a slow PE (what shows it there is the length of the first Q, 2.05; a granted clock is on record only from 18.1 us on, and the 1.00 that the page prints ahead of that is no reading); it took 8.0, and 5.7 with PE kept busy (14.85 to 20.53 in e2). The rival "PE goes cold" was priced for the middle, where it never came (granted clock 1.00 from 20 us on). It came in the start: PE is idle for 1.3 ahead of 9.06 and for 3.4 ahead of 13.24, and the clock of 10 to 15 and 15 to 20 us falls to 0.79 and 0.52. So the walk held most of this cost already, but as if it were fixed; e2 took out 1.7 in the profile and 2.2 in the median.

**The sum.** First M 2.0, body 4.2, make the last result 6.2 late; the store took 0.3 less than the 3.4 forecast, 0.3 more lay outside the span, and the 0.7 of hand-offs added at the end had come in the walk's own waits: 80.5 + 6.2 - 0.3 + 0.3 - 0.7 = 86.0, the profiled 85.9. The medians say the same: e5, without the two named causes, is at 81.53.

**What the range missed.** It carried a rival for POOL, one for PE's clock, and none for ACT, though ACT got more new work than any engine but POOL. The trace before had no row of ACT with such a walk from which to take 1.1 to 1.2; that there was none was the reason to keep a wide end there.

The best kernel of the study is e15 (79.53, and 79.47 when run again: 0.845, 0.840 to 0.849), the changed kernel with the walks in pairs, warming matmuls, x0 and x1 loaded first, and the tail of e8: 7 us under the changed kernel and 14 under the one before. e12 to e14, e16 and e18 leave work out and are no kernels to use.

## What to carry to other kernels

Price a new copy by its walk through memory, not by its size alone: 512 elements cost ScalarE 0.63 to 0.74 in pairs and 1.10 to 1.20 one by one. Look first whether the old kernel had the cheaper order. When a change hands work to an engine that had room on average, walk that engine through the last fifth of the kernel as well: in this kernel results, seeds and copies fall together there. To learn what holds an end, read who each engine waits for once one of them is relieved, and relieve that one too. And where a change takes work away from TensorE, look for the stretch in which it now sits idle ahead of matmuls that the rest waits for, and read the granted clock of the stretch behind it.

## What the runs showed of the hardware that was not expected

- The order of the walk: ScalarE's 512-element seed (SBUF to PSUM) 1200 ns against 740, its result (PSUM to SBUF) 1102 against 625, VectorE's result 1097 against 690, with the same elements and only the order changed.
- A load of 192 KB issued ahead of one of 512 KB: the statistics that wait for the large one start at 7.1 to 8.3 in twelve profiles, and at 5.6 (e15, e18) with the large one first. With 0.5 KB more between them they start at 8.51 and 8.75 (e9, e10), two executions only.
- PE idle for 1.3 and 3.4 us in the start, and a granted clock of 0.52 in the stretch behind; with fillers 1.00 in four profiles of seven.
- From one execution of the same kernel to another, the start alone moves by over a microsecond (first M at 19.55 in e15 and 18.24 in e17), while from first M to last result they differ by 0.03. For an edit of the body the difference within the profile is the finer measure.
